# Eight full expert tiles of the first three batches run before the last batch's rows, lists and tile table are there

## The reference, cut to what matters

```
t = t + FFN(layernorm(t)):
logits = flat @ Wr                      # 4096 tokens, 8 experts
top_vals, top_idx = top_k(logits, 2)
for e in range(8):
    hdn = gelu(flat @ W1[e] + b1[e])    # 256 -> 1024
    y = hdn @ W2[e] + b2[e]             # 1024 -> 256
    out = out + gates[:, e:e + 1] * y
```

## Time and profile before

| | |
|---|---|
| Median of 3 runs | 1321.52 us (1319.78 to 1323.84) |
| The profiled execution, its own time | 1325.95 us |
| Its span | 1324.1 us |
| PE busy in the span | 1149.3 us (87%) |
| DVE, ACT, POOL busy | 794.7, 628.5, 578.6 us |
| Mean clock granted to PE | 0.94 of full |

### The profile page before, as it was taken

How to read it: one execution, slowest core, us unless ns; L and a number is a source line. 1 busy time by engine, 2 the same in 40 slices (tenths; PEclk the granted TensorE clock), 3 DMA queues, 4 the chain that set the end, 5 groups by cost and what they waited for, 6 DMA issues and landing times.

```text
span 1324.1 us, 29284 instructions
## 1 busy us (share of the span) xinstructions
PE 1149.3 (87%) x10343; PEld 756.3 (57%) x10343; DVE 794.7 (60%) x1425; ACT 628.5 (47%) x1129; POOL 578.6 (44%) x455
## 2 busy tenths in 40 slices
PE   3999698996679999989999998239999999999993
PEld 2454353643334444445444544139999999998772
DVE  2546546565578878868877881735555555555540
ACT  0636356462347756765676676313333333333332
POOL 1313224231348865276347617343444445444430
PEclk9989899896769999999999999769999999999996
DMA  4116653343412323232242301812333333332227
GB/s 123 48 64 207 269 163 90 116 144 97 159 32 63 78 74 74 74 90 86 50 106 76 108 29 57 322 33 34 49 49 50 49 50 50 50 52 42 42 30 261
DMA packets 99247, 120.47 MB, mean 91 GB/s; under 512 B 29401, under 2 KB 76441, under 8 KB 98489
## 3 DMA queue, kind: packets, MB, share of 16 engines
q1 hardware_dynamic: 78152, 70.29, 17.9%
q0 software_dynamic: 20544, 42.22, 14.3%
q10 hardware_dynamic: 432, 6.29, 1.2%
HBM read 72.97 MB, written 45.60 MB: 90 GB/s over the span
## 4 chain that ended last, share of the span: by engine, by line
PE 74%; DVE 8%; DMA 5%; ACT 5%; issue 4%; DVEq 2%; SPq 1%; POOL 1%; PEldq 0%; PEld 0%; ACTq 0%; POOLq 0%
PE PP L894 23%; PE PP L1242 14%; PE PP L1130 9%; PE PP L1104 8%; PE PP L966 3%; PE PP L1063 3%; PE PP L932 3%; PE PP L1114 3%; PE PP L1119 2%; DVE mxp L1447 2%; PE PP L1019 2%; ACT WB L821 1%; DVE WORK L1366 1%; PE PP L1215 1%; DMA q_lo_d<-WORK 1%
## 5 line engine op out<-in xcount | busy, mean ns | idle before, releaser
L821 ACT ACTIVATE WB<-PP 128x512 f32<-128x512 f32 x512 | 268.4, 606 | 175.5 <-PE PP L1130 175.4
L1447 DVE TENSOR_REDUCE mxp<-PP 128x2 f32<-128x1024 f32 x256 | 301.3, 1218 | 67.5 <-PE PP L1063 65.8
L866 ACT ACTIVATE WORK<-PP,b1c 128x256 f32<-128x256 f32 (+1 forms) x320 | 141.2, 449 | 260.6 <-PE PP L894 235.9
L631 POOL TENSOR_TENSOR WB<-WB 128x1024 f32<-128x1024 f32 x80 | 188.6, 2358 | 80.0 <-PE PP L1119 71.7
L894 PE MATMUL PP<-WORK,WB 128*128 128x256 f16 (+1 forms) x1920 | 207.7, 264 | 3.2 <-DVE WORK L1748 3.1
L1242 PE MATMUL PP<-WB,WORK 128*128 x1704 | 193.8, 273 | 0.0
L894 PEld LDWEIGHTS PP<-WORK,WB 128*128 x1920 | 176.5, 98 | 29.6 <-issue 4.3
L1242 PEld LDWEIGHTS PP<-WB,WORK 128*128 128x128 f16 x1704 | 164.4, 98 | 20.9 <-issue 0.4
L1130 PE MATMUL PP<-WORK 97*128 97x256 f16 x1024 | 159.9, 280 | 15.9 <-ACT WB L821 12.2
L599 POOL TENSOR_TENSOR WB<-WORK,WB 128x1024 f16<-128x1024 f32 x32 | 68.1, 2128 | 226.7 <-ACT WORK L732 226.7
L695 POOL DMA_INDIRECT res_d<-WORK,lb x71 | 116.8, 1645 | 104.2 <-DVE WORK L1775 86.3
(11 more groups left out here) (250 smaller groups left out, 1166.7 us busy)
## 6 DMA issues: line engine op xcount, KB each, us to landing
WORK<-in_L_ffn_W_dram POOLq DMA_DIRECT2D x32, 512.0 KB, 4.3
res_d<-WORK SPq DMA_DIRECT2D x8, 1024.0 KB, 4.5
late_d<-WB POOLq DMA_DIRECT2D x1, 6144.0 KB, 18.8
WB<-late_d ACTq DMA_DIRECT2D x3, 2048.0 KB, 17.7
WORK<-in_x_dram SPq DMA_DIRECT2D x8, 512.0 KB, 3.6
v_d<-WORK SPq DMA_DIRECT2D x4, 1024.0 KB, 4.7
WORK<-q_hi_d SPq DMA_DIRECT2D x16, 256.0 KB, 3.9
WORK<-v_d SPq DMA_DIRECT2D x8, 512.0 KB, 5.6
```

Of the source, the lines that this page charges most:

```text
L631: pool.tensor_tensor(PS[n % 2], PR[n % 3][:, 0], PR[n % 3][:, 1], ALU.add).then_inc(s("pair_kept"), 1)
L821: act.activation(PR[n % 3][:, c // 2, c % 2 * 2:c % 2 * 2 + 2], SCORES[m % 3] .rearrange("p (h n) -> p h n", h=2), ACT.Exp).then_inc(s("e_ ...
L866: act.activation(hid[u][:, k, 0:width], hidden_bank(k)[:, 0:width], ACT.Gelu, bias=b1c[:, bass.ds(e, 1), k], scale=1.0 / WSCALE)\
L1447: dve.tensor_reduce(mxp[:, n // 4 % 2, i, h:h + 2, k], PP[2 + h // 2][:, :].rearrange("p (h n) -> p h n", h=2), X_AXIS, ALU.max).then_inc( ...
```

## The change

A table for eight early tiles (`EARLY`) is made in steps 21 to 27 of the last batch's attention, from the counts of batches 0 to 2, and only of lists that are full to 256 tokens by then. These tiles 0 to 7 are run first. Beside and between them go the last batch's norm (ACT), low halves (DVE), scatter (POOL) and the table for the other 32 tiles (DVE). The number of tiles, 40, stays. The rows of batch 2 are stored earlier, in the last batch's attention. `hid` has one buffer in place of two. The tile loops of ACT and DVE are written out in full in place of loops over registers. New or moved code:

```
 SP, attend(3), k == 7, behind the load of t1:
+                    if k == 7 and last:
+                        store_rows(b - 1, b)
 SP, after attention:
+            sp.wait_ge(s("early_kept"), 1)
+            sp.wait_ge(s("st_list"), 16 * 2 * NT * (B - 1))
+            for t in range(LISTS):
+                load_list(t)
+            store_res1(B - 1, B)
+            sp.dma_start(b2b, ...).then_inc(s("ld_b2"), 16)
+            store_rows(B - 1, B)
+            for t in range(LISTS, EARLY):
+                load_list(t)
+            (waits for res1, rows, lists, table; then lists 8 to 39)
 POOL:
-            scatter(B, range(2 * NT))
+            def last_pieces(i):
+                for j in (i, i + 2):
+                    scatter(B, range(j, j + 2))
+                    pool.wait_ge(s("st_list"), 16 * (2 * NT * (B - 1) + j + 2))
+            pool.wait_ge(s("st_rows"), 16 * (B - 1))
             for t in range(3):
                 gather(t)
+            last_pieces(0)
             for t in range(TILES):
                 if t + 3 < TILES:
                     gather(t + 3)
                 store_output(t)
+                if t < 3:
+                    last_pieces(4 * (t + 1))
 ACT:
-            (norm of all eight token tiles, wait for table_kept)
+            act.wait_ge(s("early_kept"), 1)
+            for t in range(TILES):
+                if t == EARLY:
+                    act.wait_ge(s("table_kept"), 1)
+                gelus(t)
+                if t == 0:
+                    act.wait_ge(s("st_res1"), FREE + 16 * B)
+                if t < NT // 2:
+                    norm_pair(t)
 gelus(t):
+                    if t and k % 2 == 0:
+                        act.wait_ge(s("hs_kept"), FREE + 4 * (t - 1) + k // 2 + 1)
 PE, in attend(3), step 21: tail_count, one product of ones16 and held16
 PE, after the eight tail_project:
-            tail_ranks(B - 1, FINAL_SLOTS, B)
-            (count; wait for table_kept)
             turn(0, 0, rows_loaded(0))
+            tail_ranks(B - 1, FINAL_SLOTS, B)
+            pe.wait_ge(s("early_kept"), 1)
+            pe.wait_ge(s("ld_last"), 16 * LATE)
             for t in range(TILES + 1):
+                if t == EARLY - 1:
+                    pe.wait_ge(s("table_kept"), 1)
                 (first(t), turn(t + 1))
+                if t == 0:
+                    (the count of all four batches)
                 (second(t - 1))
 DVE, in attend(3), steps 21 to 27: early_table, seven parts of
 one to four operations on at most 128x64 elements
 DVE, after the statistics:
+            keep_turned(0, 0)
             (tail_pick, tail_rstd, tail_places, tail_gates)
+            split_hidden(0, 0)
+            keep_turned(1, 1)
+            for t in range(TILES):
+                e = expert(slice(t, t + 1))
+                if t == 0: (copy of the count)
+                split_hidden(t + 1, (t + 1) % 2, t + 1 < PAIRS)
+                if t < NT // 2:
+                    tail_low(t)
+                keep_turned(t + 2, t % 2, t + 2 < PAIRS)
+                keep_output(t, t % 2, e, t, t < PAIRS)
+                if t == 1:
+                    count_lists()
+                if t == 2:
+                    place_pairs()
+                if t == 3:
+                    singles_near()
+                if t == 4:
+                    singles_far()
```

More of the change, by code:

```diff
@@ L28 @@
 TILES = PAIRS + SINGLES
+EARLY_MAX = (2 * (B - 1) * N - E * (TT - 1)) // TT
 REGION = B * N + TT
@@ L619, in _ @@
                 pool.memset(two4[:, k:k + 1], float(2 * k + 2))
+            for k in range(E):
+                pool.memset(seq8[:, k:k + 1], float(k))
             pool.memset(step8, 0.0)
@@ L849, in _, with norm_pair @@
             tail_gate(B)
[L850 to L863, removed]
+            def norm_pair(part):
+                for t in (2 * part, 2 * part + 1):
+                    op = act.activation(t1[:, t], t1[:, t], ACT.Identity,
+                                        bias=small[:, 4, t:t + 1], scale=small[:, 3, t:t + 1])
+                op.then_inc(s("ln1_kept"), 1)
+                tail_high(part, B, t1[:, 2 * part:2 * part + 2])
@@ L1093, in tail_ranks, with tail_count @@
                 mm.then_inc(s("c_made"), 1)
+            def tail_count(b, before, n):
+                bank = next_slot(b, before)
+                pe.wait_ge(s("idx_kept"), FREE + n)
+                product(bank[:, 0:E], [(ones16[:, :], held16[:, :])], "c_made")
             def weigh_heads(n):
@@ L1163, in attend @@
                             tail_ranks(b, before, b)
+                        if last and t == COUNT_AT:
+                            tail_count(b, before, b)
             for name, n in (("vt_kept_v", 1), ("vt_kept_a", 1), ("qlo_kept", 4)):
@@ L1588, in attend @@
                         tail_gates(b - 1, b)
+                    if last and t in EARLY_AT:
+                        early_table(EARLY_AT.index(t), before)
             for n in range(4):
@@ L1606, in _ @@
             slots[0] = 0
[L1607 to L1625, removed]
@@ new lines, in tail_low @@
+            def tail_low(part):
+                here = slice(2 * part, 2 * part + 2)
+                dve.wait_ge(s("hi_kept"), 4 * (B - 1) + part + 1)
+                dve.tensor_tensor(rows[:, here, 1, :], t1[:, here], rows[:, here, 0, :], ALU.subtract)\
+                   .then_inc(s("rows_kept"), 1)
+            for c in range(NT):
+                tail_project(c, before, B)
+                tile_statistics(c)
+            dve.drain()
+            deviations("stat1_kept")
+            keep_turned(0, 0)
@@ L1783, in _ @@
+            for part in range(4):
+                tail_pick(part, B)
+            tail_rstd(B)
+            tail_pick(4, B)
+            for part in range(3):
+                tail_places(part, before, B)
+            tail_gates(B - 1, B)
             split_hidden(0, 0)
             keep_turned(1, 1)
-            with dve.Fori(0, (PAIRS - 1) // LISTS) as i:
-                for j in range(LISTS):
-                    u, t = j % 2, i * LISTS + j
-                    e = expert(bass.ds(t, 1))
-                    dve.wait_ge(s("y_made"), FREE + t)
-                    split_hidden(t + 1, 1 - u)
-                    keep_turned(t + 2, u)
-                    keep_output(t, u, e, j)
```

375 lines of the change are left out of this document (209 added, 166 removed).

## The result

The changed kernel took **1327.9 us** (median of 5, 1324.71 to 1332.01), the kernel before 1321.52 (5 runs). The ratio is 1.0055, 95% interval 1.0032 to 1.0079: slower by half a per cent, 6.4 us by the medians. The forecast was 1324.5, range 1312 to 1333. Its working can be checked term by term in the profile after, so that is what follows.

What follows compares the result with a forecast made beforehand. Bounds: a hole before tile 0, then PE's loop with POOL close behind. 1325.95 - 23.8 (start) + 23.2 (scatters) + 1.4 (table) + 1.9 (clock) + 0.3 (attention) = 1328.95; the profiled run lay 4.4 above the median, so 1324.5 us, range 1312 to 1333.

Steps and rivals of the forecast that it cites:

- What bounds: End of attention onward: a hole before tile 0, slow tiles 0 and 1, then PE's 10.93 us a tile, POOL close behind.
- Part 2: Tiles 0 to 6: four scatters behind each of three adds delay gathers 4 to 6; PE waits 7.0, 8.1, 8.1, 23.2 us lost.
- Part 4: PE behind the three new waits: low clock, absorbed behind the first two, costing 1.9 us behind the third.
- Part 1: Start of tile 0: first(0) at 856 instead of 879.74, 23.8 us gained, with small transfers slowed by the late weights.
- Part 3: Table code on DVE: three pieces hidden by POOL's waits, singles_far exposed at tile 7, 1.4 us lost.
- rival C: Table code on DVE is the wait: written-out code pauses, 3.5 us more at tile 7, 1328.0 us; chance 0.20.
- signs that the prediction named: Next profile: first(0) at 855 to 858, list loads of 10 us or more, three PE waits of 7 to 8 us.
- one sign against it: The prediction is wrong if gathers 4 to 6 are issued on time, or if tile 0 starts before 852.
- A (small transfers pass): Before tile 0: small transfers pass beside the weights, first(0) at 849, gain 30.7 instead of 23.8, 1317.6 us; chance 0.18.
- B (scatters hide): Tiles 0 to 6: scatters do not hold PE, so their loss and the clock's vanish, 1299.4 us; chance 0.08.

Runs made afterwards that it cites:

- e1_ahead: Changed kernel with all 16 scatters of the last batch issued ahead of the tile loop, none between adds and gathers: 1308.19 us, ratio 0.9928.
- c2_after: The changed kernel, unedited, measured and profiled once more on the same chip as a repeat of the kernel before: 1328.2 us, ratio 1.0088.
- e4_rows: Changed kernel with only the store of batch 2's rows put back behind the last spread of inverse sums on SP's queue: 1326.42 us, ratio 1.0062.
- e9_between: Changed kernel with only batch 2's rows stored between the 4 KB store of inverse sums and their broadcast: 1324.3 us, ratio 1.0051.

## Why the prediction was right, and where its terms were off

**What bounds, and the shape of the account: right.** A gain of some 20 us ahead of tile 0, given back by POOL within six tiles. The undoing of the second half alone (e1_ahead) shows it.

**Part 2, POOL: right in mechanism; the sum fits by two errors that cancel, which is luck.** Forecast 23.2 and 1.9 for the clock, measured 25.5. A pair of scatters was priced at 4.8 us and took 4.45 in the mean of six. Against that the last add of the three landed 2.3 us later than usual, while SP's 1 MB of rows was being stored. That the move of `store_rows(3)` into the tile loop would meet an add was not in the sum. The spare time of POOL in a tile is 10.93 - 9.3 = 1.6 us rather than the 2 that was written, which changes nothing here.

**Part 4, the clock: right.** The prediction's 1.9 sets 7.09 of PE's timeline against 5.24 of the chain; like for like, 7.09 against 5.40, it is 1.7. Behind the three waits the output took 2.2, 1.7 and 1.7 us more than 5.40, and the turn 0.4 more behind the first and the third. The first two are absorbed by POOL's pace, as forecast: turns 4, 5 and 6 stand 17.8 and 20.8 us apart, and POOL's cycles were 17.6 and 21.1. The second wait is 4.14 and not 8.1 as the cycle was 17.8 us and not 19.0, and as PE was at work for 13.7 us of it and not 10.93, at the low clock for a part. A wait of 2 us is not always followed by the low clock: behind the 2.22 us ahead of 861.38 the granted clock was 1.00 and the hidden layer took 5.45, where c2_after has 7.11 behind 2.13 us.

**Part 1, the start: the term that was mis-sized.** 23.8 forecast, 20.3 and 21.0 measured (first and second pair of traces). The one-for-one turns of small packets with the weights, taken from the earlier trace rows, were right, and e4_rows shows them for elements of 12 bytes as well. The route was another than forecast. The prediction put 8 rows of the broadcast on each of 16 engines and list 0 behind them, landing 16.0 us after attention's end (844.6 less 828.58). In fact the broadcast had 32 rows on each of four engines, and normalise ran 13.9 us after attention's end where it had run at 2.0: 12 later, not 3 to 8. List 0 landed at 14.0, and what held the gathers was normalise, which stands ahead of them in POOL's order. That gather 0 was nevertheless issued by 17.8, against 18.3 forecast, is luck. The term that was mis-sized stands behind it: rows 0 were to be there 2.2 us after that issue, a time taken from the kernel before, where no weights were in flight, and the weights were to be "covered". But the third load, late with normalise, was in flight, and the rows took 5.8. So the start missed by 3.4 us (30.8 against 27.4): 3.6 for the rows, 0.4 for `keep_turned`, picks and ranks, less the 0.6 by which the gather was early. e4_rows and e9_between do take the forecast's route, through list 0, and reach 31 us as well.

**Part 3, the table: right.** 1.4 forecast, 1.9 measured. `singles_far` ran without the pauses, 943.4 to 948.2. So rival C did not happen. e1_ahead shows the piece that was said to be hidden, 1.44 us at tile 4.

**The signs that the prediction named.** Turn(0) ended by a DMA from `rows_d`, four scatters between add and gather, waits at three turns and none from turn 7 on, the low clock behind each: all seen. The waits were 6.7, 4.1 and 8.1 us, so the second lies outside "7 to 8", and the list loads took 3.0 to 9.2 us, not 10 or more. By the letter one sign against it came true: tile 0 starts at 850.40, before 852. That number was counted from the start of the span, and attention ended 9.0 us earlier in this trace; counted from attention's end the forecast was 27.4 and the start came at 30.8, later and not earlier.

**Rivals.** A (small transfers pass) fell: the broadcast, the lists and the gathers were all held up. B (scatters hide) fell, but it names the change that pays: e1_ahead. The packet rule of the Trainium skill ("DMA: Bandwidth & Descriptors", section on queues, rings and completion order) says that a DMA engine takes turns between queues, and the trace agrees: 64 packets against 64. It also gives a packet some 9 to 17 descriptors; that does not hold here, where in e4_rows 52 elements of 12 bytes met 52 pieces of 16 KB.

## What to carry to other kernels

When work is moved into a loop to hide it, look at the spare time of the engine that issues it, in that loop, and not at how busy it is over all: POOL was 44% busy here and had less than 2 us to spare in a tile. Each wait for a landing on such an engine counts as its work; put the DMAs where the engine is idle and let the consumer wait for them. And do not put many small transfers into the time of a few large ones, even on another queue: here they went packet for packet, and a chain of small ones (broadcast, list, gather) paid at every link. When several such links end at nearly the same time, mending one of them alone shows nothing, as e4_rows and e9_between do.

## What the runs showed of the hardware that was not expected

- Elements of 12 bytes on one queue and pieces of 16 KB on another took turns one for one (52 and 52 in 834 to 836 us of e4_rows). The first 256 elements needed 9.5 us there, in which 3.9 MB of weights passed.
- The broadcast, whose source has an outermost dimension of 4, used four of the 16 DMA engines: 9 of its rows passed in 2 us beside 67 packets of the weights.
- A load of 2 MB that started alone landed in 8.0 us, where one issued behind two others had taken 21.1; it had the DMA engines almost to itself, with only gathers beside it.
- An add into DRAM landed 2.3 us later while 1 MB of rows was being stored, in four traces alike (waits of 5.46 to 5.50 us; in the first of them the other adds have 3.1 to 3.4).
